# Four images of linear attention in one staggered stage, and the tally of clipped edges inside the fourth layer's stream

## The chip, the core and the metric

One core of a Trainium2 chip runs the whole program. The metric is the device time of one execution in microseconds. Engines are called TensorE (PE; its weight loads PEld), VectorE (DVE), ScalarE (ACT), GpSimd (POOL) and SyncE (SP, which only issues transfers here).

## The reference, cut to what matters

The input has 4 images of 128 channels by 32 x 32, which become 1024 tokens of 128 numbers each. Four layers follow one another; these lines of the reference carry the parts that the change touches:

```python
# third layer: linear attention, then a mixture
k = _inst_norm(k); v = _inst_norm(v)
dots = jnp.einsum('bhnd,bhne->bhde', k, v)
out = jnp.einsum('bhnd,bhde->bhne', q, dots) * (1.0 / n)
t = t + out_as_tokens @ w_out + b_out        # t: the tokens; q, k, v from _ln_t(t)
# fourth layer: attention over all tokens and in a window, then a graph attention
loops = jnp.arange(M, dtype=edge_index.dtype)
src = jnp.concatenate([edge_index[0], loops])
dst = jnp.concatenate([edge_index[1], loops])
e = jax.nn.leaky_relu(a_src[src] + a_dst[dst], negative_slope=0.2)
denom = jax.ops.segment_sum(ee, dst, num_segments=M)
agg = jax.ops.segment_sum(msg, dst, num_segments=M)
```

The graph attention has 524288 edges drawn over 32768 nodes, of which the kernel has M = 4096. A source beyond the last node is clipped to the last one, so the kernel doesn't handle such edges one by one: it counts, for each of its own nodes, how many clipped edges arrive there. That count is the tally. It depends on the edge list alone, not on any layer's values.

## The kernel before, in words

Each `stage` (L37) is a block of programs, one per engine, with semaphores of its own; all engines meet at its end. `loop` (L61) is a loop on the chip with barriers. Within a stage each engine runs its instructions strictly in the order written. `Beside` (L143) writes several programs into one engine's order by the turn numbers that they yield.

*Linear attention* (`linear_attention`, L1241, called in a loop over 4 images). Per image: `layer_norm` (L443: statistics, root, normalising on VectorE L464, transposes on TensorE), then keys and values of 8 token tiles (L1262, 128x512 each, a bank of PSUM for each of them), copied and squared on ScalarE (L1276, L1277), summed per head (L1285) and all 512 columns scaled (L1291) on VectorE, products of keys and values (L1268), then three `product_pass` stages: with the output weights (L1297), with the query weights (L1303), with the tokens (L1311) plus the bias as a product with a row of ones (L1312). VectorE adds the result to the tokens (L1315), and a second `layer_norm` follows. That is seven stages an image. After the loop come `mixture_weights` and `batch_normed_mixtures`.

*Fourth layer* (`fourth_layer`, L1552). A small stage first: POOL fills `f_v_ext` with ones (L1561) and reduces two counts over the partitions (L1562, L1565), VectorE fills a row of `f_stacks` and `f_pads` (L1570, L1571) and works out the number of laps, TensorE makes one column of bias (L1579). Then one long stage, `fourth_layer_stream` (L1589), for all images: 256 steps of two half steps. In a half step TensorE makes scores into a ring of two banks (L1825), VectorE takes their maximum (L2150), TensorE makes the transposed scores (L1849), ScalarE their exponential (L2033), and TensorE multiplies with the values (L1866). Beside them, at turn numbers (one turn is a half step, an image has 128), run `pre` of the next image (norm, queries, keys, values), `local` of this image (the windowed attention) and `tail` of the image before. `pre(0)` stands ahead of the stream: statistics on VectorE (L2053), root on POOL (L2188), normalising on ScalarE (L1901), products on TensorE (last L1710), roundings, and transfers to `f_stacks`. Then come the first 32 scores.

*Slots* (`take_in_slots`, L2945). POOL gathers 128 columns of rows by indirect transfers (L2816), in four groups of 32. ScalarE packs each group (L2826), and VectorE works through it as a band (`Taking.band`, L2834: from L2839 to L2878; 33 instructions). Between bands 1 and 2 come `Refill.place` (from L2934) and the start values (to L3053). The tally stands first in VectorE's and TensorE's order of this stage: the list of clipped edges, 1024 columns of two digits, is cut into 8 chunks of `TALLY` = 128; VectorE makes 64 one-hots a chunk (L3020, two chunks buffered), TensorE multiplies high by low digit, 128 products of 64x64 a chunk (L2985), and two copies, a product and a copy spread the counts (L3033, L2991, L3035). Then `Refill.draw` (L2921), the bands and the rest follow.

Of the kernel before, what the change touches and what calls it, by code (L numbers as in the profile page):

```python
# [1240 lines left out]
def linear_attention(nc, k, b):  # L1241

    with ExitStack() as c:
# [3 lines left out]
        G = 16  # L1247
        t_tm, xn, xc = k.t_tm[:, b], sb("l2_xn", [P, NT, P]), sb("l2_xc", [P, N])
        kv, sq = sb("l2_kv", [P, NT, 4 * P]), sb("l2_sq", [P, NT, 4 * P])
        st = sb("l2_st", [P, NT, G])  # L1250
        dots, mo, g = sb("l2_dots", [P, 2, P]), sb("l2_mo", [P, 2, P]), sb("l2_g", [P, P])
        ps = c.enter_context(psum(nc, "l2_ps", [P, 8, BANK], F32))
        layer_norm(nc, k, t_tm, xn[:], ps=ps, turned=xc)
        with stage(nc, "kv_ready", "copied", "squared", "chained", "rooted", "normed", "dots_ready", "masked") as (
                block, kv_ready, copied, squared, chained, rooted, normed, dots_ready, masked):
            def heads(x, t):
                return x[:, t].rearrange("p (g d) -> p g d", d=32)

            @block.tensor
            def _(pe):  # L1260
                for t in range(NT):
                    nc.tensor.matmul(ps[:, t], chunk(xc, t, P), k.w_kv[:], start=True, stop=True).then_inc(kv_ready, 1)  # L1262

                pe.wait_ge(squared, NT)
                for t in range(NT):
                    pe.wait_ge(normed, t + 1)
                    for i in range(2):
                        last = nc.tensor.matmul(ps[:, i, 0:P], kv[:, t, (2 + i) * P:(3 + i) * P],  # L1268
                                                kv[:, t, i * P:(i + 1) * P], start=(t == 0), stop=(t == NT - 1))
                last.then_inc(dots_ready, 1)  # L1270

            @block.scalar
            def _(act):
                for t in range(NT):
                    act.wait_ge(kv_ready, t + 1)
                    nc.scalar.copy(kv[:, t], ps[:, t]).then_inc(copied, 1)  # L1276
                    nc.scalar.activation(sq[:, t], ps[:, t], ACT.Square).then_inc(squared, 1)  # L1277
# [311 lines left out]
def fourth_layer_stream(nc, k, f, c):  # L1589
# [97 lines left out]
    def _(pe):  # L1687
# [154 lines left out]
        def scores_transposed(s, n):  # L1842
            h, m = steps[s]
            i = NC2 * s + n
            if m == 0 and n == 0:
                pe.wait_ge(rows_off, h + 1)
# [1429 lines left out]
```

## Time and profile before

| | us |
|---|---|
| three runs | 2886.87, 2897.33, 2886.83; median 2886.87 |
| the profiled execution | 2889.75, of which the span of the core 2888.0 |
| linear attention, four images | about 196 |
| small stage of the fourth layer | about 13 |
| opening, to the first score | about 52 |
| stream, image 0 from the first score | about 188 |
| slots | about 369 |

| engine | busy us | share of the span | instructions |
|---|---|---|---|
| PE | 1869.1 | 65% | 8280 |
| DVE | 1648.0 | 57% | 3684 |
| ACT | 966.2 | 33% | 1542 |
| POOL | 658.1 | 23% | 675 |

No engine is busy over the whole span; each stage has a limit of its own. Times in the profile are from the span's start. Matmuls are pipelined and their ends modelled, so TensorE's busy time is not time at its peak. Its clock has two levels, 1.2 and 2.4 GHz; "PEclk" is the granted share of the higher one.

### The profile page before, as it was taken

The numbers are of one execution on the slowest core, as the hardware profiler recorded it, in microseconds if no ns is written. First come the engines' busy times: TensorE is split into PE (matmuls) and PEld (weight loads), VectorE is DVE, ScalarE is ACT, GpSimd is POOL, SyncE is SP. The second block draws the span as 40 slices with busy tenths as digits, with TensorE's granted clock in tenths as the row PEclk, the third lists the DMA queues.
The fourth block names the chain that finished last, engine by engine and source line by source line (L and its number), as shares of the span: only waits on it lengthen the run. The fifth ranks groups of instructions, "written<-read, shape, count | busy, mean of one in ns | idle before, by whom it ended". The sixth has DMA issues, their size and how long they took to land. (4 is left out here: it accounts for less than half of the span.)

```text
span 2888.0 us, 25863 instructions
## 1 busy us (share of the span) xinstructions
PE 1869.1 (65%) x8280; PEld 825.4 (29%) x8280; DVE 1648.0 (57%) x3684; ACT 966.2 (33%) x1542; POOL 658.1 (23%) x675
## 2 busy tenths in 40 slices
PE   1564893785686666599658888787886410190089
PEld 1121321321221334456312223232222210090034
DVE  3485776767768654466545756656562121088823
ACT  1232141142132131255326675665664210000133
POOL 2200600420330300044312132332123157500000
PEclk7686896787888776699859999998897655555589
DMA  3301201201200000020021110110000021100030
GB/s 86 80 18 28 59 2 43 58 0 39 50 15 18 7 0 0 0 86 18 14 66 35 27 56 14 30 42 25 24 5 9 5 63 10 8 8 31 2 124 22
DMA packets 58242, 88.62 MB, mean 31 GB/s; under 512 B 17992, under 2 KB 29250, under 8 KB 57866
## 3 DMA queue, kind: packets, MB, share of 16 engines
q1 hardware_dynamic: 47604, 77.66, 9.0%
q10 hardware_dynamic: 6426, 7.99, 1.3%
q0 software_dynamic: 4096, 1.58, 0.8%
q8 instruction: 54, 0.88, 0.1%
q14 instruction: 62, 0.51, 0.1%
HBM read 58.59 MB, written 24.74 MB: 29 GB/s over the span
## 5 line engine op out<-in xcount | busy, mean ns | idle before, releaser
L2150 DVE TENSOR_REDUCE f_half_max<-f_ring 128x1 f32<-128x512 f32 x512 | 334.8, 684 | 306.3 <-PE f_ring L1825 304.1
L2033 ACT ACTIVATE f_probs<-f_ST 128x512 f32<-128x512 f32 x512 | 293.0, 597 | 212.4 <-PE f_ST L1849 208.2
L1825 PE MATMUL f_ring<-f_stacks 96*128 96x512 bf16 x512 | 212.7, 417 | 54.4 <-DVE f_half_max L2150 27.6
L772 DVE TENSOR_REDUCE att_half_max<-att_ring 128x1 f32<-128x512 f32 x256 | 161.1, 683 | 101.4 <-PE att_ring L659 92.7
L1849 PE MATMUL f_ST<-f_stacks 99*128 99x512 bf16 x512 | 203.8, 404 | 11.6 <-ACT f_probs L2033 11.6
L2985 PE MATMUL ts_ps<-ts_tally 128*64 128x64 bf16 x1024 | 97.5, 357 | 167.4 <-issue 145.3
L755 ACT ACTIVATE att_probs<-att_ST 128x1024 f32<-128x1024 f32 x128 | 129.4, 1024 | 155.8 <-PE att_ST L684 155.6
L3020 DVE TENSOR_SCALAR ts_tally<-ts_digits 128x256 bf16<-128x256 bf16 x512 | 77.4, 231 | 166.4 <-PE ts_ps L2985 112.8
L1459 POOL TENSOR_TENSOR bm_h<-bm_h,bm_mix 128x512 f32<-128x512 f32 x64 | 82.2, 1305 | 316.6 <-DMA bm_mix<-mix 229.5
L1866 PE MATMUL f_O<-f_probs,f_v_ext 128*32 128x512 f32 x1024 | 153.0, 673 | 0.0
L2985 PEld LDWEIGHTS ts_ps<-ts_tally 128*64 128x64 bf16 x1024 | 91.9, 263 | 172.9 <-issue 150.8
L684 PE MATMUL att_ST<-stacks 96*128 96x512 bf16 (+1 forms) x512 | 137.5, 397 | 0.0
L702 PE MATMUL att_O<-att_probs,v_ext 128*64 128x512 f32 x512 | 131.9, 641 | 6.6 <-DVE att_den L791 6.6
L659 PE MATMUL att_ring<-stacks 96*128 96x512 bf16 x256 | 104.3, 473 | 46.6 <-DMA stacks<-parts_dram 25.9
L2816 POOL DMA_INDIRECT ti_row<-features,slot_from x128 | 121.5, 949 | 56.6 <-issue 56.6
L1100 DVE TENSOR_TENSOR loc_weighed<-loc_wide,l_pad 128x512 f32<-128x512 f32 x200 | 124.4, 683 | 13.6 <-PE loc_wide L1054 8.6
L2359 PE MATMUL gm_ps<-xn_cm,x 128*128 128x512 f32 x128 | 62.5, 614 | 99.6 <-PEq L43 99.6
L1436 ACT ACTIVATE bm_h<-bm_ps,bn 128x512 f32<-128x512 f32 x128 | 99.6, 778 | 78.0 <-PE bm_ps L1403 72.7
L1825 PEld LDWEIGHTS f_ring<-f_stacks 96*128 96x128 bf16 x512 | 50.6, 99 | 259.6 <-DVE f_half_max L2150 163.6
L1082 POOL TENSOR_TENSOR loc_partial<-loc_partial,loc_weighed 128x512 f32<-128x512 f32 x88 | 110.1, 1272 | 9.9 <-DVE loc_weighed L1100 6.5
L1060 PE MATMUL loc_acc<-loc_weighed,turned 128*128 128x512 f32 x208 | 107.0, 598 | 0.4
L934 POOL MEMSET loc_padded<- 104x1296 f32 x4 | 4.7, 1178 | 446.7 <-POOLq L43 446.7
(546 smaller groups left out, 3419.6 us busy)
## 6 DMA issues: line engine op xcount, KB each, us to landing
f_stacks<-f_parts SPq DMA_DIRECT2D x192, 64.0 KB, 2.2
gates_wide<-gates SPq DMA_DIRECT2D x16, 512.0 KB, 12.3
parts_dram<-l_parts SPq DMA_DIRECT2D x8, 768.0 KB, 4.1
stacks<-parts_dram SPq DMA_DIRECT2D x24, 256.0 KB, 9.4
stacks<-parts_dram ACTq DMA_DIRECT2D x24, 256.0 KB, 10.6
f_parts<-f_parts SPq DMA_DIRECT2D x8, 768.0 KB, 3.5
es_raw<-L_ffn_edge_index SPq DMA_DIRECT2D x8, 512.0 KB, 4.7
bm_mix<-mix SPq DMA_DIRECT2D x8, 512.0 KB, 9.6
```

What stands on the lines that cost most here:

```text
L684: last = nc.tensor.matmul(ST[:, s % 2, n * BANK:(n + 1) * BANK], k.stacks[0:rows, 1, per * h + j, m * P:(m + 1) * P], k.stacks[0:rows, 0, ...
L702: last = nc.tensor.matmul(O[at:at + width, :], k.v_ext[:, m, h, :], probs[:, s % probs_ring, n * BANK:(n + 1) * BANK], start=(m == 0), sto ...
L755: nc.scalar.activation(probs[:, s % probs_ring, :], ST[:, s % 2, :], ACT.Exp).then_inc(probs_ready, 1)
L772: nc.vector.tensor_reduce(half_max[:, h % 2, t, n:n + 1], ring[:, i % RING], AX.X, ALU.max, negate=True).then_inc(reduced, 1)
L1100: nc.vector.tensor_tensor(o_, a, v, ALU.mult).then_inc(weighed_ready, 1)
L1825: nc.tensor.matmul(ring[:, i % RING], f.stacks[0:STACK, 0, at, t * P:(t + 1) * P], f.stacks[0:STACK, 1, at, n * BANK:(n + 1) * BANK], star ...
L1849: nc.tensor.matmul(ST[:, i % HALVES], f.stacks[0:STACK + 3, 1, h % HEADS, m * P:(m + 1) * P], f.stacks[0:STACK + 3, 0, h % HEADS, n * BANK ...
L1866: last = nc.tensor.matmul(O[at:at + 32, :], f.v_ext[:, h // HEADS % 2, m, h % HEADS, :], f.probs[:, s % PROBS, n * BANK:(n + 1) * BANK], s ...
L2033: nc.scalar.activation(f.probs[:, s % PROBS, n * BANK:(n + 1) * BANK], ST[:, i % HALVES], ACT.Exp).then_inc(probs_ready, 1)
L2150: nc.vector.tensor_reduce(f.half_max[:, h % 2, t, n:n + 1], ring[:, i % RING], AX.X, ALU.max, negate=True).then_inc(reduced, 1)
L2816: self.nc.gpsimd.indirect_dma_start(self.row[:, j, :], None, self.k.features, bass.IndirectOffsetOnAxis(ap=self.k.slot_from[:, j:j + 1], a ...
L2985: last = nc.tensor.matmul(ps[64 * a:64 * a + 64, 0, 0:64], low, high, start=(s == 0 and m == 0), stop=(s == chunks - 1 and m == TALLY // 2 ...
```

## The change

Linear attention of all images becomes one stage, `linear_attentions`, without the loop. Each image's program is written out for each engine with turn numbers from 0 to some 520, and the next image's begins 190 later; the engines' orders are merged by these numbers. Normalising is on ScalarE; keys and values use two banks of PSUM; key and value scales are multiplied, and only the key half is scaled; the bias is copied once to all partitions and added to the tokens by POOL.

The small stage of the fourth layer is dropped and its work put into the stream's stage: POOL fills `v_ext` first, then after `pre(0)` the row of `f_stacks`, the reductions, and, behind a wait for the first five chunks of the tally, `f_pads`.

The tally leaves the slots. Its first 640 columns are counted in five chunks of 128 in the opening: VectorE makes them behind its part of `pre(0)`, TensorE multiplies them in `first()`, behind `pre(0)` and ahead of the first score. The other 384 are counted in four chunks of 96 beside image 0, with one buffer. The core of the diff:

```diff
+class Linear:
+    STAGGER = 190
+    TURNED = (80, 500)
+    def start(self, program):
+        return Beside(*((b * self.STAGGER, program(b)) for b in range(B)))
...
+def linear_attentions(nc, k):
...
+                    if i >= 2:
+                        pe.wait_ge(kv_off, 2 * (i - 1))
+                    nc.tensor.matmul(kv_ps[:, i % 2], chunk(xc, t, P), k.w_kv[:], start=True, stop=True).then_inc(kv_ready, 1)
...
+                        last = nc.scalar.activation(f.xn[:, w, t, :], k.t_tm[:, b, t, :], ACT.Identity, bias=s[:, t, 2:3],
+                                                    scale=s[:, t, 1:2])
...
+                nc.gpsimd.tensor_tensor(x, x, f.bias[:].unsqueeze(1).broadcast_to([P, NT, P]), ALU.add).then_inc(biased.sem, 1)
...
+    EARLY, EARLY_TALLIES, LATE, LATE_TALLIES, LATE_TURNS = 128, 5, 96, 4, 28
...
+        def first():
+            for s in range(f.EARLY_TALLIES):
+                yield 22 + 2 * s
...
+                pe.wait_ge(hot_ready, 64 * (s + 1))
+                multiply(O, f.hot[:, s % 2], range(f.EARLY // 2), s == 0, s == f.EARLY_TALLIES - 1).then_inc(multiplied, 1)
+
+        def tally():
+            half, per = f.LATE // 2, 4
+            for s in range(f.LATE_TALLIES):
+                for g in range(half // per):
+                    yield f.LATE_TURNS * s + 15 + g
...
+        for s in range(f.EARLY_TALLIES):
+            if s >= 2:
+                dve.wait_ge(multiplied, s - 1)
+            one_hots(f.hot[:, s % 2], f.digits[:, :, s * f.EARLY:(s + 1) * f.EARLY], range(64))
...
+            per = 5
+            for s in range(f.LATE_TALLIES):
+                for g in range(0, 64, per):
+                    yield f.LATE_TURNS * s + 1 + g // per
...
+        split.wait(pool, 0)
+        nc.gpsimd.memset(f.stacks[STACK:STACK + 3, 1], 1.0).then_inc(made, 1)
...
+        pool.wait_ge(multiplied, f.EARLY_TALLIES)
+        nc.gpsimd.memset(f.pads[:], 0.0).then_inc(cleared, 1)
...
-            for s in range(chunks):
-                pe.wait_ge(hot_ready, 64 * (s + 1))
...
-                for v in range(64):
-                    nc.vector.tensor_scalar(hot[:, s % 2, :, :, v, :], here, float(v), None,
-                                            ALU.is_equal).then_inc(hot_ready, 1)
...
-            with loop(nc, 0, B) as b:
-                linear_attention(nc, k, b)
+            linear_attentions(nc, k)
```

## Rows read from the trace of the kernel before

**Rows 1.** Page, part 2: granted TensorE clock in 40 slices of 72.2 us.

```profile
PEclk7686896787888776699859999998897655555589
```

**Rows 2.** Busy by stage: PE, PEld, DVE, ACT, POOL us (instructions), clock, DMA share, GB/s.

```profile
1015.00:1211.00 196.00, 124.17 (x416) 81.17 (x416) 96.39 (x297) 48.54 (x96) 0.00 (x0) 0.67 0.00 0
...
1424.50:1477.00 52.50, 14.55 (x33) 7.01 (x34) 2.89 (x20) 12.25 (x20) 11.22 (x17) 0.50 0.15 47
1477.00:1665.00 188.00, 159.21 (x732) 41.51 (x732) 128.52 (x272) 105.82 (x191) 34.66 (x31) 0.88 0.13 36
...
2345.80:2714.90 369.10, 98.59 (x1028) 92.83 (x1028) 189.50 (x710) 13.18 (x13) 121.46 (x128) 0.50 0.11 21
```

**Rows 3.** Busy time by stretch: the first image of linear attention.

```profile
1015.00:1064.00 49.00, 30.78 (x104) 20.10 (x104) 24.37 (x75) 12.07 (x24) 0.00 (x0) 0.69 0.00 1
```

**Rows 4.** Groups of instructions, second image: busy us, mean ns, idle before them.

```profile
L1262 PE MATMUL l_ps<-w_kv,l_xc 128*128 128x512 f32 x16 | 8.5, 693 | 1.0 <-PEq L43 1.0
L1312 PE MATMUL l_ps<-rows,ones_row 1*128 1x128 f32 x16 | 6.0, 475 | 0.0
...
L1291 DVE TENSOR_TENSOR l_kv<-l_kv,l_st 128x512 f32<-128x512 f32 x8 | 4.9, 684 | 0.0
...
L464 DVE TENSOR_SCALAR l_xn<-t_tm,ln_s 128x128 f32 x16 | 4.3, 346 | 0.1
```

**Rows 5.** Timeline, fourth layer's opening: start, us, engine, line, operation [idle before].

```profile
1412.12 3.51 POOL L1561 MEMSET f_v_ext<- 128x4096 f32 x1 [3.29 <-ACTq L43]
...
1424.64 1.65 DVE L2053 BATCH_NORM_STATS2 f_moments_pre<-t_tm 128x6 f32<-128x128 f32 x8 [0.92 <-PEq L1582]
...
1432.06 0.20 POOL L2188 TENSOR_TENSOR f_norm_pre<-f_norm_pre 128x8 f32<-128x8 f32 x1 [10.01 <-issue]
...
1435.81 3.19 ACT L1901 ACTIVATE f_xn<-t_tm,f_norm_pre 128x128 f32<-128x128 f32 x8 [28.71 <-POOL f_norm_pre L2192]
...
1455.80 2.07 PE L1710 MATMUL f_side<-turned,xn_cm 128*128 128x128 f32 x8 [0.69 <-ACT f_v_ext L163]
...
1476.98 0.13 PEld L1825 LDWEIGHTS f_ring<-f_stacks 96*128 96x128 bf16 x2 [19.41 <-DMA f_stacks<-f_parts]
```

**Rows 6.** Busy time by stretch, in the slots.

```profile
2363.00:2426.00 63.00, 7.20 (x35) 4.94 (x33) 11.94 (x48) 2.10 (x1) 47.55 (x51) 0.50 0.15 10
2426.00:2526.00 100.00, 10.55 (x39) 7.39 (x40) 0.00 (x0) 0.00 (x0) 61.25 (x65) 0.50 0.12 8
2526.00:2603.00 77.00, 76.82 (x919) 76.61 (x918) 65.03 (x397) 0.00 (x0) 0.00 (x0) 0.50 0.05 19
```

**Rows 7.** Timeline of the slots.

```profile
2349.84 12.65 DVE L3020 TENSOR_SCALAR ts_tally<-ts_digits 128x256 bf16<-128x256 bf16 x80 [3.17 <-DMA ts_digits<-last_digits]
...
2389.03 2.10 ACT L2826 COPY ti_packed<-ti_row 128x768 f32<-128x768 f32 x1 [50.62 <-DMA ti_row<-features,slot_from]
...
2505.82 0.95 POOL L2816 DMA_INDIRECT ti_row<-features,slot_from  x1 [0.30 <-issue]
...
2539.02 8.81 DVE L3020 TENSOR_SCALAR ts_tally<-ts_digits 128x256 bf16<-128x256 bf16 x64 [1.95 <-PE ts_ps L2985]
...
2647.44 1.86 DVE L2934 TENSOR_REDUCE rf_fresh<-rf_drawn 128x32 f32<-128x1024 f32 x1
...
2668.00 0.42 DVE L2839 TENSOR_TENSOR ti_hot<-tiles,slot_tile 128x256 f32<-128x256 f32 x1
...
2714.37 0.23 DVE L2941 COPY slot_from<-rf_from 128x128 int32<-128x128 int32 x1
```

**Rows 8.** Busy time by stretch, in image 0 of the stream.

```profile
1517.00:1556.00 39.00, 32.62 (x162) 11.50 (x162) 18.58 (x36) 27.43 (x50) 6.38 (x3) 0.96 0.06 21
1556.00:1594.00 38.00, 34.16 (x182) 8.85 (x178) 22.43 (x43) 25.12 (x44) 13.10 (x6) 1.00 0.15 46
```

**Rows 9.** Busy time by stretch of L2033 alone, in image 0.

```profile
1556.00:1594.00 38.00, 18.25 (x32) 1.00 0.15 46
```

**Rows 10.** Groups of instructions, 1556 to 1665 us: one of POOL's.

```profile
L2213 POOL TENSOR_TENSOR f_prod<-f_lq,f_pads 128x1024 f32<-128x1024 f32 x5 | 11.0, 2210 | 9.1 <-PE f_side L1728 9.1
```

More of the change, by code:

```diff
@@ L1674, in fourth_layer_stream, with starts @@
     LAYER = [(0, 0), (1, 0), (0, 1), (1, 1)]
-    def starts(pre, local, tail):
-        programs = [(0, pre(0))]
+    def starts(pre, local, tail, first=None, tally=None, others=()):
+        programs = [(0, pre(0))] + ([] if first is None else [(0, first())])
+        head = len(programs)
+        if tally is not None:
+            programs.append((0, tally()))
+        programs.extend((0, other()) for other in others)
         for b in range(B):
@@ L1869, in mix @@
             last.then_inc(mixed_ready, 1)
-        before, beside = starts(pre, local, tail)
+        before, beside = starts(pre, local, tail, first, tally)
         before.finish()
@@ L1925, in pre @@
                 yield 20 + 2 * u
+                if b == 0 and u == 0:
+                    act.wait_ge(made, 1)
                 heads = f.v_ext[:, b % 2, 4 * u:4 * u + 4, :, 0:HD]
@@ new lines, in laps @@
+        def laps():
+            yield 10
+            dve.wait_ge(laps_reduced, 2)
+            count_laps(nc, k, linker(dve, laps_counted))
+        before, beside = starts(pre, local, tail, None, tally, (laps,))
+        before.finish()
+        for half in range(2):
+            r = slice(64 * half, 64 * half + 64)
+            nc.vector.tensor_copy(f.place[r, :], k.ident[r, r]).then_inc(tally_made, 1)
+        nc.vector.memset(f.total, 0.0).then_inc(tally_made, 1)
+        dve.wait_ge(digits_in, 32)
@@ L2169, in _ @@
+        dve.wait_ge(multiplied, f.EARLY_TALLIES)
+        for odd in range(2):
+            nc.vector.tensor_copy(f.total[:, odd, :, odd], O[:, 0:64]).then_inc(counted, 1)
         for s in range(len(steps)):
@@ L3030, in _ @@
             refill.place(dve, link, spread)
-            dve.wait_ge(multiplied, chunks)
-            for odd in range(2):
-                nc.vector.tensor_copy(total[:, odd, :, odd], ps[:, 0, 0:64]).then_inc(counted, 1)
-            dve.wait_ge(placed, 1)
-            link(nc.vector.tensor_copy(count[:], ps[:, 1, 0:MT]))
-            link(nc.vector.tensor_scalar(last[:, 0], count[:], 0.5, NEG, ALU.is_lt, ALU.mult))
+            link(nc.vector.tensor_scalar(last[:, 0], k.count[:], 0.5, NEG, ALU.is_lt, ALU.mult))
             for h in range(GH - 1, -1, -1):
```

420 lines of the change are left out of this document (289 added, 131 removed).

## The prediction, made before the changed kernel was run

> **What bounds the kernel now.** I read first where the granted clock is low (the page's slices), then the span by stage, then inside each stage the edit touches the timeline. The low-clock slices [rows 1] are the places where TensorE waits or does little: the linear attention, the opening of the fourth layer and the whole intake of slots. The stages give the sizes [rows 2]: linear attention 196 us, opening 52.5, first image 188, slots 369. No engine fills the first of these: an image takes 196/4 = 49.0 us, in which TensorE is busy 30.8, VectorE 24.4, ScalarE 12.1 [rows 3]; it is one chain, cut into seven small stages, in a loop. In the opening VectorE has 2.9 us of work in 52.5 [rows 2]. In the slots the tally is the plug: VectorE makes its one-hots ahead of everything else in its queue, and all four bands of slots come behind it. After 80 fast one-hots [rows 7] it gives out 48 in 63 us, and TensorE does 74 products and no more in 163 us [rows 6]; no wait on another engine is shown, and it ends some 20 us after the last gather is issued at 2505.82 [rows 7]. Then 919 products take 76.8 us [rows 6]. So the stage has three pieces in a row: tally beside the gather at a crawl, tally, bands.
>
> **Part 1, linear attention: -88 us.** Removed: the loop with its barriers, six stage boundaries an image, the bias products of each token tile (L1312, 6.0 us an image), half of the scaling (L1291, 4.9 us to about 2.8, since the two scales are multiplied) [rows 4]. Added: normalising goes from VectorE to ScalarE, twice 3.19 us [rows 5] against twice 2.15 [rows 4]; POOL adds the bias beside the keys and values, off the path (1024 columns took it 2.2 us elsewhere [rows 10]). The chain of one image: 49.0 - 6.0 - 2.1 + 2.1 - 5 for boundaries (the products of L1262 sat 1.0 us behind one of them [rows 4]; the rest is an estimate) + 2 for keys and values through two banks instead of eight, about 40 us. The next image starts 190 units of some 520 behind, which is 15 us of such a chain, so engines set the pace: ScalarE 12.1 + 6.4 = 18.5, VectorE 24.4 - 4.3 - 2.1 = 18, TensorE 30.8 - 6.0 = 24.8 at a clock of 0.67 to 0.69 and less when it is higher [rows 2 to 4]. I take 22. The stage: 40 + 3 x 22 + 2 to start = 108, against 196. Ends: 40 + 3 x 18.5 = 96 (-100); all at 1.2 GHz TensorE's 24.8 us become 24.8 x 0.67/0.50 = 33 an image, the chain about 46: 146 (-50).
>
> **Part 2, opening of the fourth layer: +19 us.** The small stage (13 us from the end of the mixtures at 1411.5 to 1424.6) goes. Its 3.5 us of filling v_ext [rows 5] stays on POOL ahead of the root, but the two all-reduces are moved behind; POOL's root began 7.4 us after VectorE's first statistics, with 10 us of idle before it that no wait explains [rows 5], and now can begin 4 us after. So TensorE's part of pre(0), which ended at 1457.9, ends at about 1412 + 33.3 - 3.5 = 1442. Now the tally: VectorE makes chunks 0 and 1 (64 x 0.138 = 8.8 us each [rows 7]) from 1416 to 1434, then waits for TensorE, which has first() behind all of pre(0) and ahead of the first score. A chunk of 128 products cost 76.8/919 x 128 = 10.7 us, and the clock stayed at 0.50 with TensorE busy without a gap [rows 6]; so five take 1442 + 53.5 = 1495.5, and the one-hots of the later chunks (8.8) fit beside. The first score comes at 1495.7 instead of 1476.98 [rows 5]: +19. If the clock were 1.0, VectorE would bind: 1442 + 5.3 + 3 x 8.8 + 5.3 = 1480, +3. High end +26: the root no earlier, and the stacks' row of ones (filled by VectorE before, now by POOL) in the way. SP issues two digit loads ahead of all its others; before, the one-hots began 4.0 us after their stage, so their load is short [rows 2, 7], and no stack load is due for 45 us. Queued behind POOL's new wait for the fifth chunk is the root of pre(1), not due before the stream has run six half steps: nothing.
>
> **Part 3, late tally beside image 0: +28 us.** 256 one-hots of 192 columns, between 0.103 and 0.138 us: 26 to 35 us of VectorE, and 384 products of 0.042 (half of the measured 0.084) to 0.084: 16 to 32 us of TensorE [rows 6, 7]. A half step, one exponential, takes 38/32 = 1.19 us [rows 9] with TensorE busy 34.2 of 38 and VectorE 22.4 [rows 8]. The one-hots come 5 to a half step in 13 of 28 half steps: 0.70 + 0.60 = 1.30 us, over 1.19, and the ring of two banks hands each delay to TensorE: 6 to 20 us over 52 half steps. The products, 8 to a half step over 48, find 10% slack, 6 us: 10 to 26. Together 16 to 46, I take 28; range 8 (busy figures overstate TensorE) to 60.
>
> **Part 4, slots: -180 us.** What is left for VectorE: the draw, two bands, the placing, the start, two bands. A band takes 46.4/2 = 23.2 us (2668.00 to 2714.37), placing and start 20.6 less 1.5 for the removed copies and product (2647.44 to 2668.00) [rows 7]. Band 0 can begin when ScalarE has packed it, 2389.0 + 2.1 = 2391 [rows 7]; bands 0 and 1 end at 2437, placing and start at 2457; band 2 waits for its gather, near 2469 + 2, and ends at 2494. Group 3 lands some 2.4 us after 2505.8 + 0.95 (group 0's last gather, 96 of 1.25 us earlier, ended at 2386.6, its pack began at 2389.0), is packed at 2511.3, and the last band's remaining 22.2 us end at 2534. The stage ended at 2714.6: -180. Late next is the gather itself. The stake is the crawl: VectorE then got one instruction in 63/48 = 1.3 us [rows 6]. It needs some 75 by the end of band 1 and had 80 ahead of the crawl; if all had to come at that rate, two bands of 33 take 66 x 1.3 = 86, placing and start 43 x 1.3 = 56, to 2533; two bands at speed follow: 2580, -134.
>
> By the Trainium skill ("Runtime: NRT & Kernel Launch", Instruction fetch mechanics) an engine holds 512 instructions, TensorE 2048, refilled in blocks, and a taken branch breaks the prefetch. No run here shows the buffer; the crawl after 80 instructions speaks for a fetch, and for rival C below.
>
> **Sum.** 2889.75 (the profiled execution, span 2888.0) - 88 + 19 + 28 - 180 = 2668.75; the median of the runs is 2.9 lower, so 2666.
>
> **The rivals.**
> A, as above: 2666. Chance 0.54.
> B, the tally holds TensorE at 1.2 GHz beside image 0. For it: 77 us without a gap left the clock at 0.50 [rows 6]. Against: the stream raised it to 0.96 by 1517 to 1556 [rows 8]. At half the clock 34.2 us of work in 32 half steps becomes 68: +0.97 us a half step, over the 48 with products +47: 2713. Chance 0.12.
> C, the crawl takes VectorE's bands: 2666 + 46 = 2712. Chance 0.13.
> D, POOL and VectorE block each other in image 0: POOL is busy 34.7 us there [rows 2], in ops of up to 2.2 us [rows 10]; if each that falls in the one-hots' 46% of half steps holds VectorE back, +16: 2682. Chance 0.08. The Trainium skill ("SBUF — State Buffer", Who interferes with whom) has tensor_scalar in its fast mode and POOL exclude each other for a whole instruction. Beside the gather 80 one-hots took 12.65 us, 0.158 each against 0.138 alone [rows 7]: a small cost, so the trace gives the rule little.
> E, the opening runs at full clock and the late tally hides: -16 - 20: 2630. Chance 0.07.
> F, the stagger doesn't overlap, because an in-order queue waits for the older image: 4 x 40 = 160 in part 1, +52: 2718. Chance 0.04. Against: the waits on older images are for buffers two images back or for banks long emptied.
> G, slower: the clock stays at 0.50 through the fourth layer's stream, since the tally both precedes and accompanies it. At 0.97 us a half step it eats the 221 us of gain after 228 half steps of 512, 1.8 images; for the whole stream +497: 3163. Against: the clock of [rows 8], and the tally ends within image 0. Chance 0.02.
>
> **How the numbers follow.** Range: A spreads by its own ends (about -35 and +45 combined), B, C, F lie inside 2740, E above 2625; so 2625 to 2740. 0.5% is 14 us, about what a measurement of this kernel can tell from no change; only G and rests of combined mishaps reach above 2872: faster 0.97, same 0.01, slower 0.02.
>
> **What would show it.** Part 1: from the first statistics of linear attention to the mixture weights near 108 us, one table load, ScalarE or TensorE busy over 80% in the middle. Part 2: five chunks 10.7 us apart at clock 0.50, first score 84 us after the end of the mixtures. Part 3: image 0 from 188 to some 216 us, and its clock (B). Part 4: first band right behind the first pack, last band ending 25 us after the last gather is issued; instructions spaced 1.4 us would be C. The forecast fails if the bands crawl and the clock drops together, or if the gather itself grows longer with bands beside it.

## The result and the profile after

The changed kernel takes 2757.34 us (median of 4 runs, 2752.18 to 2763.18) where the kernel before took 2886.85 (4 runs): ratio 0.9545, 95% interval 0.9526 to 0.9564. I had forecast 2666, with a range of 2625 to 2740. The direction was right; the gain was 130 us instead of 221, and the time lies outside the range. The profiled execution has a span of 2761.5 us against 2888.0. By stage, from the first statistics of linear attention to the choice of experts:

| stage | before | after | change | forecast |
|---|---|---|---|---|
| linear attention | 195.2 | 122.6 | -72.6 | -88 |
| mixtures | 200.4 | 201.1 | +0.7 | 0 |
| opening, to the first score | 65.5 | 86.7 | +21.2 | +19 |
| image 0, first score to its fourth group | 187.8 | 249.3 | +61.5 | +28 |
| images 1 to 3 | 561.9 | 567.7 | +5.8 | 0 |
| slots, last group to choice of experts | 491.2 | 349.4 | -141.8 | -180 |

This was not the whole result. On another chip the same two kernels gave 2726.75 us (10 runs) against 2734.46 (13 runs): ratio 0.9975, interval 0.9959 to 0.9991. Next to no gain is left there, and the experiments show why.

The page of the changed kernel, granted TensorE clock in 40 slices of 69 us, answers to [rows 1]; busy time by stretch, columns as in [rows 2], answers to [rows 2] and [rows 8]. In order: an image of linear attention, twice; the opening; its second half, with the tally alone; image 0 to its first group, and the rest of it.

```profile
PEclk7696787888689688799758989989989865555599
```

```profile
1040.00:1068.00 28.00, 17.18 (x85) 12.20 (x83) 17.86 (x57) 16.41 (x38) 3.01 (x2) 0.80 0.00 1
1068.00:1096.00 28.00, 17.18 (x82) 12.16 (x82) 17.80 (x57) 16.18 (x38) 2.34 (x1) 0.80 0.00 1
...
1338.00:1390.00 52.00, 35.84 (x286) 28.58 (x288) 32.59 (x198) 12.29 (x20) 23.79 (x20) 0.52 0.19 62
1390.00:1425.00 35.00, 32.91 (x393) 32.53 (x390) 20.18 (x149) 0.00 (x0) 11.75 (x2) 0.50 0.22 61
...
1425.00:1516.00 91.00, 75.79 (x340) 24.26 (x338) 65.04 (x208) 36.67 (x65) 11.18 (x17) 0.75 0.03 9
1516.00:1674.00 158.00, 138.06 (x784) 46.64 (x780) 105.89 (x326) 71.60 (x125) 26.01 (x15) 0.87 0.08 23
```

In the middle of linear attention no engine is busy for more than 18 of 28 us, so none of them sets the pace. VectorE's last copy of each of the four images (its timeline) shows how they follow one another:

```profile
1074.24 0.69 DVE L1470 COPY xn_cm<-l_turn 128x512 f32<-128x512 f32 x1 [0.22 <-PE l_turn L1301]
1102.75 0.69 DVE L1470 COPY xn_cm<-l_turn 128x512 f32<-128x512 f32 x1 [0.22 <-PE l_turn L1301]
1123.52 0.69 DVE L1470 COPY xn_cm<-l_turn 128x512 f32<-128x512 f32 x1
1136.09 0.69 DVE L1470 COPY xn_cm<-l_turn 128x512 f32<-128x512 f32 x1 [4.43 <-PE l_turn L1301]
```

The stage began at 1014.55, so the images end 60.4, 88.9, 109.7 and 122.2 us after its start. The opening's tally runs with a single gap, of 2.1 us, at clock 0.50, as [rows 6] had it. In image 0 TensorE has 213.9 us of work where it had 159.2 [rows 2], and its clock is low again for stretches.

The slots of the changed kernel, timeline of VectorE (start us, us, engine, line, operation, idle before and what ended it), answer to [rows 7]:

```profile
2408.29 1.23 DVE L3112 TENSOR_TENSOR ti_z<-ti_hot,ti_packed 128x1024 f32<-128x1024 f32 x1 [23.42 <-issue]
...
2449.07 1.23 DVE L3112 TENSOR_TENSOR ti_z<-ti_hot,ti_packed 128x1024 f32<-128x1024 f32 x1 [17.39 <-ACT ti_packed L3083]
...
2491.71 0.23 DVE L2993 TENSOR_SCALAR rf_from<-rf_whole 128x128 int32<-128x128 int32 x1 [1.16 <-DVE rf_whole L2992]
2493.12 0.26 DVE L2994 TENSOR_SCALAR rf_whole<-rf_whole 128x128 int32<-128x128 int32 x1 [1.18 <-DVE rf_from L2993]
2494.51 0.23 DVE L2995 CAST rf_f<-rf_whole 128x128 f32<-128x128 int32 x1 [1.13 <-DVE rf_whole L2994]
...
2541.69 0.43 DVE L3096 TENSOR_TENSOR ti_hot<-tiles,slot_tile 128x256 f32<-128x256 f32 x1
...
2588.09 0.23 DVE L3198 COPY slot_from<-rf_from 128x128 int32<-128x128 int32 x1
```

Band 0 and band 1 run at full speed as soon as they are packed; placing and start, between them and 2541.7, come for the most part one instruction in 1.40 us, although most of them take a quarter of a microsecond. I call that the crawl. The last gather is issued at 2525.6, the crawl ends some 13 us later, and bands 2 and 3 then stand behind it. That is rival C's cause in another place: C had bands 0 and 1 crawl too, and they didn't.

### The profile page after: what moved, and what is told of

It is laid out like the page before. It is cut to its first block and busy times, and to the rows that moved or that the text cites. A ratio compares the mean times of both kernels' runs of the same rounds, so it can differ in the third digit from the quotient of the medians.

```text
span 2761.5 us, 25395 instructions
## 1 busy us (share of the span) xinstructions
PE 1840.1 (67%) x8218; PEld 792.3 (29%) x8218; DVE 1628.0 (59%) x3680; ACT 990.0 (36%) x1604; POOL 693.1 (25%) x681
## 5 line engine op out<-in xcount | busy, mean ns | idle before, releaser
L2015 PE MATMUL f_ring<-f_stacks 96*128 96x512 bf16 x512 | 217.2, 425 | 44.8 <-DVE f_half_max L2351 38.7
L2061 PE MATMUL f_O<-f_probs,f_v_ext 128*32 128x512 f32 x1024 | 161.2, 706 | 0.1
L2015 PEld LDWEIGHTS f_ring<-f_stacks 96*128 96x128 bf16 x512 | 51.0, 100 | 250.1 <-DVE f_half_max L2351 167.2
L2617 PEld LDWEIGHTS gm_ps<-xn_cm,x 128*128 128x128 f32 x128 | 25.2, 198 | 306.7 <-issue 306.7
L2670 DVE TENSOR_TENSOR gm_h<-gm_h,gates_wide 128x1024 f32<-128x1024 f32 x32 | 39.2, 1226 | 98.3 <-ACT gm_h L2655 98.3
L912 PE MATMUL loc_ps<-loc_prod,place 128*32 128x512 f32 (+1 forms) x208 | 54.9, 688 | 32.8 <-DVE loc_prod L958 32.8
```

The lines of the kernel that those rows point to most:

```text
L2015: nc.tensor.matmul(ring[:, i % RING], f.stacks[0:STACK, 0, at, t * P:(t + 1) * P], f.stacks[0:STACK, 1, at, n * BANK:(n + 1) * BANK], star ...
L2061: last = nc.tensor.matmul(O[at:at + 32, :], f.v_ext[:, h // HEADS % 2, m, h % HEADS, :], f.probs[:, s % PROBS, n * BANK:(n + 1) * BANK], s ...
L2617: nc.tensor.matmul(ps[:, g % HIDDEN], k.x1[:, e, half * P:(half + 1) * P], chunk(k.xn_cm[:, b], n), start=True, stop=True).then_inc(hidden ...
```

## The experiments

The 18 runs below are in five groups, each on one chip with its own executions of the kernel before. A kernel without an interval was executed once. Times of stages are read from one profile each; a stage that an edit leaves alone came out within 1.5 us in nearly all of them (the opening at 86.4 to 86.8), but images 1 to 3 took 557 to 570 without a pattern. That kernel took 2730.89 in the first, 2734.46 in the second, and 2891.31, 2886.21 and 2890.86 us in the third to fifth. So there are chips where it takes some 2731 us and chips where it takes some 2888, and which it is matters more than the change. I call the second kind the chips with the crawl. No chip was used in two of the groups, so the chip and its state at that time can't be told apart.

### Group 1: image 0 taken apart (no crawl)

```diff
-                    last = multiply(x0.psum, f.hot_late, range(per * g, per * (g + 1)), s == 0 and g == 0,
-                                    s == f.LATE_TALLIES - 1 and g == half // per - 1)
+                    if g == 0:
+                        last = multiply(x0.psum, f.hot_late, range(per), s == 0, s == f.LATE_TALLIES - 1)
```

> Leaves out 88 of every 96 late products (352 of 384), so the edge counts are incomplete; all one-hots stay. Image 0 of the fourth layer (first score to the end of its fourth group) took 249.3 us in the changed kernel against 187.8 before, 61.5 more where I forecast 28. Theory: in the half steps with products TensorE is the bound, and eight products add their full 0.82 us (0.103 each, seen at full clock), so without them image 0 falls by some 36 us, to about 213. Rival one-hots: VectorE's bursts are the cost, and image 0 falls by under 10, to 240 or more. Rival clock: the low clock that lasted until the late tally's end comes from the products, and image 0 falls by over 45, to under 204.

```diff
-                    one_hots(f.hot_late, ..., range(g, min(g + per, 64)))
+                    if g == 0:
+                        nc.vector.tensor_scalar(f.hot_late[:, :, :, 0, :], here, 0.0, None, ALU.is_equal).then_inc(hot_ready, 64)
```

> Leaves out 63 of the 64 late one-hots of each chunk (the buffer is filled with zeros once by GpSimd), so the edge counts are incomplete; all 384 late products stay. Theory of TensorE's products: image 0 keeps most of its 61.5 us and falls by about 22 to 227. Rival one-hots: it falls by over 45, to 204 or less. If the one-hots hide wholly under TensorE it stays at 249.

> Leaves out both, 352 of 384 late products and 252 of 256 late one-hots. Both theories: image 0 comes back to the 187.8 us of before, give or take 4. If the two single runs gave falls that add up to this one's 61, they are independent costs; if they add to less, both must go for the time to come back. If it stays over 200, something else in the opening or the moved laps costs the rest.

Image 0 took 214.8 us without the products, 220.9 without the one-hots, 190.9 without both, against 249.3. The falls are 34.5, 28.4 and 58.4: nearly additive (62.9), so these are two costs of about the same size, and my 28 us held room for one. (Some 3 us stay: 190.9 is not 187.8.) Both "only products" and "only one-hots" are out. Busy time by stretch from the second group on, without the products, without the one-hots, without both (one row from each kernel):

```profile
1506.60:1636.60 130.00, 105.83 (x517) 26.76 (x516) 103.11 (x325) 70.19 (x126) 25.71 (x15) 0.89 0.10 28
```

```profile
1510.20:1643.60 133.40, 123.47 (x781) 45.03 (x780) 79.74 (x164) 71.13 (x126) 25.61 (x15) 0.99 0.10 28
```

```profile
1503.80:1615.00 111.20, 96.50 (x517) 25.92 (x516) 77.53 (x164) 69.74 (x126) 25.54 (x15) 0.98 0.12 33
```

With products and no one-hots the clock is 0.99; with one-hots and no products 0.89; with both 0.87. So the products don't hold the clock down, which refutes rival B as I had put it. The low stretches come with the one-hots, which make TensorE wait for its ring: in image 0 it sat idle for VectorE's maximum before its scores (L1825 before, L2015 after; idle times over 0.1 us summed) for 21.6 us with both and 24.4 without the products, and for 9.7 and 12.2 in the two kernels without the one-hots. Where the products lie, the timeline of TensorE in the changed kernel shows what they cost:

```profile
1535.71 0.89 PE L1919 MATMUL f_side<-f_hot_late 128*64 128x64 bf16 x8
1536.53 0.39 PE L2015 MATMUL f_ring<-f_stacks 96*128 96x512 bf16 x1
1536.76 0.38 PE L2042 MATMUL f_ST<-f_stacks 99*128 99x512 bf16 x1
1537.07 0.89 PE L1919 MATMUL f_side<-f_hot_late 128*64 128x64 bf16 x8
1537.89 0.39 PE L2015 MATMUL f_ring<-f_stacks 96*128 96x512 bf16 x1
```

Eight products take 1537.89 - 1537.07 = 0.82 us, 0.103 each at a clock of 1.00, more than the 0.084 that they took at 0.50 [rows 6], and a half step becomes 1.36 us. Part of that is the change from one kind of product to the other: the four pairs of the second row begin at 1537.07, 1537.28, 1537.44 and 1537.60, and the score 0.29 us after the last pair. Inside the row a pair takes 0.160 us, against 0.168 at half the clock. The 352 that were left out are 36 us, of which 34.5 reached the end: TensorE had next to no slack there.

```diff
-            for g in range(2):
-                t.band(dve, link, g, packed, shifted, exped, banded)
-            refill.place(dve, link, spread)
             (the start)
+            refill.place(dve, link, spread)
-            for g in range(2, BANDS):
+            for g in range(BANDS):
                 t.band(dve, link, g, packed, shifted, exped, banded)
```

> Slots: placing and start are moved ahead of band 0 on VectorE, into its 23.4 us of waiting for the first pack, with the start's exponential first on ScalarE; nothing is left out. Theory, crawl by count: VectorE gets about 80 instructions fast, whenever they come, and then one per 1.4 us until some 13 us after the last gather. Start, placing and band 0 (about 87 with the draw) are then fast, bands 1 and 2 crawl at 28 x 1.4 = 39 us each beside the gather and band 3 ends about 2530 + 30: the stage goes from 229 to about 200 us. Rival, crawl by place: it is the placing and start (many short instructions) that crawl wherever they stand; then they take 60 us from 2385, band 0 begins at 2445, and the stage takes 225 or more. Rival, crawl by time (it begins about 110 us into the gather whatever was issued): bands 0 and 1 are fast, band 2 crawls, stage about 195.

It took 2721.58 us, and from the first draw to the choice of experts 185.5. But the three kernels beside it that leave the slots alone took 186.0, 186.5 and 186.8 there, against 218.1 in the first profile of the changed kernel. No instruction had crawled in any of them, so this run said nothing on the order, and raised the question of the chip.

### Group 2: both kernels again (no crawl)

> The kernel before, unchanged, on a chip of its own choosing, for its profile. In the last experiments no instruction of VectorE crawled in the slots, and the kernel before took 2730.89 us there against 2886.85 in the first comparison. If the crawl belongs to the chip and not to the kernel: on a chip without it the one-hots of the tally run at 0.138 us each beside the gather, TensorE's products at 0.084, the stage of slots takes about 371 - 156 = 215 us, and all stages ahead of it are as before. If the 156 us lie elsewhere, a stage ahead of the slots is shorter.

> The changed kernel, unchanged, beside the kernel before on the same chip. If the crawl belongs to the chip: without it the slots take about 186 us (as in the three experiments that left that stage alone) and the whole some 2729, so against 2731 the change is worth nothing there, a ratio of 1.00; with it the ratio is 0.955 as in the first comparison. If it belongs to the kernels, the ratio is 0.955 on every chip.

The kernel before took 2723.23 us in its profiled execution. The stages up to the end of image 0 were as in the first profile (195.4, 200.1, 65.7, 187.6), and images 1 to 3 took 557.0 against 561.9; from the last group to the choice of experts it took 334.0 instead of 491.2. The changed kernel took 317.3 there. So where nothing crawls, moving the tally out of the slots saves 16.7 us, and it costs 21.0 in the opening and 62.8 in image 0. (By these two profiles alone the change loses 6 us, since images 1 to 3 differ by 13.1; the medians have it 7.7 ahead.) The slots of the kernel before, by stretch and in TensorE's timeline:

```profile
2363.00:2426.00 63.00, 63.00 (x761) 63.00 (x758) 58.95 (x383) 2.15 (x1) 51.42 (x39) 0.50 0.12 9
2426.00:2526.00 100.00, 12.33 (x140) 11.96 (x136) 89.37 (x162) 10.00 (x10) 72.91 (x71) 0.50 0.19 36
...
2351.62 85.64 PE L2985 MATMUL ts_ps<-ts_tally 128*64 128x64 bf16 x1024 [21.90 <-DVE ts_tally L3020]
```

All 1024 products run in one piece of 85.6 us beside the gather, where [rows 6] showed 74 in 163 us. There TensorE crawled too (its timeline, kernel before, first profile):

```profile
2385.39 0.27 PE L2985 MATMUL ts_ps<-ts_tally 128*64 128x64 bf16 x1 [2.53 <-issue]
2388.19 0.27 PE L2985 MATMUL ts_ps<-ts_tally 128*64 128x64 bf16 x1 [2.53 <-issue]
```

One product comes in 2.80 us. A product is two instructions, its weight load and itself, so that is 1.40 us an instruction again.

The tally lies beside the gather, but not for nothing. The gather took 181.9 us (2338.3 to 2520.2), against 160.2 in the crawl, and 166.7 in the changed kernel on this chip; 15.2 of the 16.7 us are this difference. Most of its calls still come 1.25 us apart, but two lasted as long as 64 one-hots. One of them, timelines of VectorE and GpSimd:

```profile
2394.61 8.81 DVE L3020 TENSOR_SCALAR ts_tally<-ts_digits 128x256 bf16<-128x256 bf16 x64 [0.63 <-PE ts_ps L2985]
...
2393.72 0.94 POOL L2816 DMA_INDIRECT ti_row<-features,slot_from  x1 [0.31 <-issue]
2394.97 8.58 POOL L2816 DMA_INDIRECT ti_row<-features,slot_from  x1 [0.30 <-issue]
2403.85 0.94 POOL L2816 DMA_INDIRECT ti_row<-features,slot_from  x1 [0.30 <-issue]
```

In these two chunks the one-hots ran at their full speed and a call waited them out (8.58 and 8.44 us instead of 0.95); in the others the calls kept their pace and 64 one-hots took 10.0 to 10.1 us. In the changed kernel the gather is the bound, and VectorE waits for the packs:

```profile
2363.00:2472.00 109.00, 0.00 (x0) 0.00 (x0) 53.06 (x74) 6.54 (x6) 83.39 (x85) 0.50 0.35 56
2472.00:2520.00 48.00, 0.00 (x0) 0.00 (x0) 37.63 (x88) 3.69 (x4) 36.99 (x37) 0.50 0.13 9
```

Up to 2472 this agrees with the first profile of the changed kernel (74 instructions against 72 in the same stretch); then 88 instructions come in 48 us where the other had 50 in 67.

```diff
-                for a in range(2):
-                    low, high = (hot[:, d, a, :, m] for d in range(2))
-                    last = nc.tensor.matmul(bank[64 * a:64 * a + 64, 0:64], low, high, ..., tile_position=(0, 64 * a))
+                low, high = (hot[:, d].rearrange("p a v m -> p (a v) m")[:, :, m] for d in range(2))
+                last = nc.tensor.matmul(bank[:, 0:P], low, high, ...)
```

> The tally's two products of 64x64 for a column (one for each half of the chunk, at two tile positions) become one of 128x128, whose two diagonal blocks are the same sums: 512 instead of 1024 products, one-hots unchanged, same result. Theory: a product costs its issue, 0.084 us in the opening and 0.103 beside the stream, with little for its columns; then image 0 falls by about half of 34.5, 17 us, and the opening's chunks cost 5.4 instead of 10.8 us of TensorE and are bound by VectorE's 8.8: about -8. Together 25 us less than the changed kernel. Rival: the cost is columns moved at 1.2 GHz (128 columns are 0.107 us), then the opening gains 0.168 - 0.107 = 0.06 a pair, hidden by VectorE, and image 0 gains as above if its clock is full. Rival no gain: weight load of 128 columns costs double, both stay.

2787.35 us, 2.1% more than the kernel before (ratio 1.0207, interval 1.0181 to 1.0233) and 60.6 us more than the changed kernel: +24.4 us in the opening and +37.2 in image 0. None of the three cases held. TensorE's timeline:

```profile
1366.19 80.78 PE L1918 MATMUL f_O<-f_hot 128*128 128x128 bf16 x320
```

One product of 128x128 takes 0.252 us at clock 0.50, two of 64x64 take 0.168. So halving the number of products is no way to make this tally cheaper: the price isn't the issue of an instruction. In the trace the two products of 64x64 of a pair, at their two tile positions, begin together, for the most part some 0.01 to 0.02 us apart. Whether the pair gains by that, or the 128x128 loses by its size or by the columns' stride in the one-hots, wasn't tried.

```diff
-                nc.gpsimd.tensor_tensor(x, x, f.bias[:].unsqueeze(1).broadcast_to([P, NT, P]), ALU.add)
+                nc.gpsimd.tensor_tensor(x[:, 0, 0:1], x[:, 0, 0:1], f.bias[:, 0:1], ALU.add)
```

> Linear attention: GpSimd's addition of the bias (1024 columns, 2.35 us an image) is cut to one column, so the output bias is missing from the tokens. In the changed kernel the 8-column scale on VectorE that falls beside it took 1.91 us where its twin took 0.17, and ScalarE's normalising waits 1.81 us for it, once an image. Theory of the shared port: the scale takes 0.2 us again, and the four images together end up to 4 x 1.8 = 7 us earlier (122.5 to about 116). Rival: the delay is off the path set by keys and values, and the stage stays within 1 us.

Linear attention took 119.1 us instead of 122.8, and all eight scales took 0.17. In the changed kernel, timelines of VectorE and of GpSimd:

```profile
1058.14 0.17 DVE L1426 SCALAR_TENSOR_TENSOR l_s<-l_s 128x8 f32<-128x8 f32 x1
...
1062.07 1.91 DVE L1426 SCALAR_TENSOR_TENSOR l_s<-l_s 128x8 f32<-128x8 f32 x1
...
1061.61 2.34 POOL L1480 TENSOR_TENSOR t_tm<-t_tm,l_bias 128x1024 f32<-128x1024 f32 x1 [20.94 <-ACT l_xn L1366]
```

The second scale ends at 1063.98, GpSimd's addition at 1063.95: it waited the addition out. That happened twice in the stage (1.91 and 1.90 us), not once an image as I had expected; two times 1.74 us are 3.5 of the 3.7 that the stage gained. At a stagger of 150 (below) none of the eight scales met an addition. The Trainium skill ("SBUF — State Buffer", Who interferes with whom) says that a VectorE instruction with two inputs in SBUF contends with a GpSimd instruction that reads SBUF; the trace agrees, 1.91 us against 0.17. I had looked for this contention in image 0 and not where the change puts a new GpSimd operation beside VectorE.

### Group 3: part 1 alone, and its stagger (crawl)

```diff
-            with loop(nc, 0, B) as b:
-                linear_attention(nc, k, b)
+            linear_attentions(nc, k)
```

> The kernel before with the staggered linear attention alone; tally, small stage and slots stay as they were. My forecast gave part 1 88 us; the profiles of the changed kernel show 72.6 fewer in that stage. Theory: the gain of that part reaches the end in full on any chip, 73 us less than the kernel before, since nothing downstream depends on it: about 2660 where the kernel before takes 2733 and no instruction crawls in the slots (ratio 0.973), about 2814 where it takes 2887. Rival: part of it is given back in the mixtures or the opening (another clock, another state of the queues), ratio over 0.98.

2817.13 us, ratio 0.9756 (0.9724 to 0.9788), 74.2 us less than the kernel before in the same group (2891.31), with the stage at 122.5. The first theory holds: part 1 reaches the end in full.

```diff
-    STAGGER = 190
+    STAGGER = 150
```

> Changed kernel with the images of linear attention 150 units apart instead of 190. If the order of the in-order queues sets the pace of 28.8 us an image (each engine is busy for only 16 to 23 of them), a closer stagger moves waits about and the stage changes by several us either way: up to 3 x 28.8 x (1 - 150/190) = 18 us shorter if the pace follows the stagger. If TensorE's work at its low clock sets the pace, it stays within 2 us of 122.7.

> The same with 240 units. If the pace follows the stagger, 3 x 28.8 x (240/190 - 1) = 23 us longer. If TensorE sets the pace, within 2 us of 122.7.

The stage took 107.5 us at 150 and 115.1 at 240, against 122.6 at 190. Both are shorter, so the pace neither follows the stagger nor is it TensorE's work: at 190 the images meet badly in the in-order queues (argued from these three times and the waits below; no run moved a single due time). At 150, by stretch:

```profile
1052.00:1075.00 23.00, 18.59 (x93) 12.88 (x92) 16.97 (x59) 16.56 (x41) 3.39 (x2) 0.93 0.00 1
```

ScalarE's first squares of the four images begin 15.2, 17.8 and 22.2 us apart, where the changed kernel has 19.0, 28.9 and 28.5. What the 190 units cost, TensorE's timeline of the changed kernel shows in one place:

```profile
1060.05 1.12 PE L1301 MATMUL l_turn<-ident,l_xn 128*128 128x128 f32 x4 [7.22 <-ACT l_xn L1366]
1064.63 2.08 PE L1323 MATMUL l_dots_ps<-l_kv 128*128 128x128 f32 x8 [3.47 <-DVE l_kv L1455]
```

TensorE waits 7.2 us for the normalising of one image and 3.5 for the scaling of another.

```diff
+            for _ in range(40):
+                link(nc.vector.memset(t.n[:, 0, 0, 0:1], 0.0))
             refill.draw(dve, link, pool_in, drawn)
```

> Changed kernel with 40 one-column fillings more on VectorE at the head of the slots, inside its wait for the pool of candidates. Where the kernel before takes 2887 (a place where instructions crawl): by the theory of a count of 80, band 0 would be the last fast one and bands 1, placing and start crawl, some 40 instructions at 1.4 us earlier; the slots grow by 15 to 40 us. Where the kernel before takes 2730 nothing crawls, and the stage stays at 186 us after the first wait, whatever the count.

The stage stayed at 218.2 us. The 40 fillings ran in 4.9 us while the gather was beginning (2350.5 to 2355.4), and the crawl began after some 105 instructions instead of some 75, ten instructions earlier in the program, at the end of band 1. So only a few of them counted; the test was badly placed and doesn't decide between count and time.

### Group 4: what the crawl hangs on (crawl)

```diff
-            for j in range(g * SLOTS, (g + 1) * SLOTS):
+            for j in range(g * SLOTS, g * SLOTS + 4):
                 self.nc.gpsimd.indirect_dma_start(...)
```

> Slots of the changed kernel with 4 of 32 gathers a band, the rest of the rows zeros, so most clipped edges are left out. Where the kernel before takes about 2890 (crawl): by the theory that the gather's own traffic slows the fetch of instructions, VectorE no longer crawls, and the stage is bound by VectorE's work, 10 for the draw + 4 x 23.2 + 20.6 = 124 us or, waiting for its inputs, up to 135. If instructions still come 1.4 us apart, the gather is not the cause. Where the kernel before takes 2730, nothing crawls and the stage is the same 124 to 135 against 197: then the gather is the bound of the stage in the changed kernel, by some 65 us.

125.9 us from draw to choice, on a chip where the kernel before took 2886: with 16 gathers instead of 128 nothing crawls. So the gather is needed for the crawl (one run). It isn't enough, since with all 128 calls the first two groups had no crawl.

> The kernel with start and placing ahead of band 0, again. Where the crawl occurs: crawl by a stock of some 80 instructions: start, placing and the first dozen of band 0 are fast, bands 0 to 2 take about 39 us each, and from the first draw to the choice of experts it takes 205 to 225 us against 218 of the changed kernel. Crawl by time (109 us after the gather's start): bands 0 and 1 fast, 190 to 200. Crawl of these instructions wherever they stand: over 225. Where nothing crawls: 185.5 as before.

2729.95 us in one run, with 194.8 from draw to choice against 218.1 (the first comparison) and 218.2 (the run with 40 fillings). VectorE's timeline:

```profile
2385.82 1.12 DVE L3260 SCALAR_TENSOR_TENSOR own_num<-ts_n,ts_last,own_num 128x32 f32<-128x32 f32 x4
...
2390.60 0.25 DVE L2982 SCALAR_TENSOR_TENSOR rf_code<-rf_fresh,band_low 128x32 f32<-128x32 f32 x1
2391.01 0.25 DVE L2983 SCALAR_TENSOR_TENSOR rf_code<-rf_code,band_low 128x32 f32<-128x32 f32 x1
2392.41 0.29 DVE L2989 TENSOR_SCALAR rf_f<-rf_code,bounds 128x128 f32<-128x128 f32 x1 [1.15 <-DVE rf_code L2983]
...
2395.90 0.23 DVE L2992 CAST rf_whole<-rf_f 128x128 int32<-128x128 f32 x1 [1.05 <-DVE rf_f L2991]
2397.30 0.23 DVE L2993 TENSOR_SCALAR rf_from<-rf_whole 128x128 int32<-128x128 int32 x1 [1.17 <-DVE rf_whole L2992]
```

The crawl now begins 38 us after the gather's start (2352.6) instead of 109, so it is no matter of time alone; the start ran fast, so it isn't these instructions. More instructions issued early bring it on early. But the stock is not a fixed 80: 83 instructions in the kernel before, some 75 with the old order, some 55 with the new one here and in one kernel below, some 30 in the other. Bands 0 to 2 beside the gather then took 44, 45 and 41 us (2402.2 to 2532.2; I had 39), and the last one ran fast. Without the crawl the same order took 185.5, so in this order the crawl costs 9 us and not 32: the packs come some 42 us apart in any case, and a crawling band takes little more.

Both combined kernels have the stagger of 150. In the one the tally is moved and start and placing come first, in the other the tally stays in the slots.

> The changed kernel with the stagger of 150 units and with start and placing ahead of band 0. Where nothing crawls: 2727 - 15 = 2712, ratio 0.992 to the kernel before, since the gather bounds the slots. Where it crawls: 2757 - 15 = 2742 and less what the new order gives in the run beside this one.

> The kernel before with the linear attention at a stagger of 150 units alone; tally, small stage and slots as they were. Where nothing crawls: 2734 - 73 - 15 = 2646, ratio 0.968, some 66 us under the moved tally, because there the tally lies beside the gather nearly for nothing. Where it crawls: 2817 - 15 = 2802, ratio 0.970, and slower than the moved tally.

2721.87 us (ratio 0.9419, 0.9378 to 0.946) and 2802.62 us (ratio 0.9714, 0.9691 to 0.9737). With the crawl the first beats both kernels of this study. The 81 us between the two are not the tally's alone, since the order differs too: the kernel with the tally moved, the stagger of 150 and the old order took 2744.36 (one run, in group 3), which leaves some 58 us for the tally and 22 for the order.

### Group 5: the same two (crawl)

> The kernel before with linear attention at a stagger of 150 alone, again. Where nothing crawls (kernel before at 2723 to 2739): 2734 - 90 = 2644, ratio 0.967. Where it crawls (kernel before at about 2886): 2802 as last time.

> The changed kernel with stagger 150 and start and placing ahead of the bands, again. Where nothing crawls: 2727 - 17 = 2710, ratio 0.991, some 66 us slower than the tally kept in the slots. Where it crawls: 2722 as last time, 80 faster than the tally kept.

The chip had the crawl again: 2801.81 (0.9706, 0.9679 to 0.9733) and 2722.87 (0.9436, 0.9408 to 0.9464), as in group 4. What the kernel with the tally kept takes without the crawl was not measured. An estimate from the stages above: 2734.46 - 72.6 - 15.1 = 2647 us, against 2712 for the moved one (2726.75 - 15.1).

## Why the prediction was wrong

- Part 1, -88, measured -72.6. That the gain reaches the end in full held, when the part ran alone. The sum behind it, a chain of 40 us and then 22 us an image, failed in both terms. The first image ended 60.4 us after the stage's start, since the others' instructions stand between its own, and the starts followed each other by 19.0, 28.9 and 28.5 us. I took the pace from the busiest engine and assumed that the written order would reach it. At 150 units the stage took 107.5, my 108, but that is luck: its first image took 60.1 too, and the others ended 22.9, 14.1 and 10.1 us apart. At the 190 of the change the order costs 15 us against that. [rows 3] and [rows 4] could not show this: the place to look was the due times in the new code, two images side by side.
- Part 2, +19, measured +21.2. Right, by its own steps: GpSimd's root began 4.3 us after the statistics, the tally ran at clock 0.50 and 0.084 us a product, and TensorE waited once, 2.1 us, for the one-hots of the third chunk. These took 12.72 us instead of 8.80: the first two, begun at 1379.9 and 1380.0, lasted 4.26 and 4.18 us, until GpSimd's fill of the stacks' row of ones (6.92 us) ended at 1384.03, and the rest ran at full speed. I had named that fill for the high end. The wait is read from the trace; no run left the fill out.
- Part 3, +28, measured +61.5, the second largest error. This step failed in both of its terms. I priced a product at 0.042 to 0.084 us, taking half of the measured 0.084 as the price at full clock. It was 0.103 at full clock (0.080 inside a row of eight), so the clock makes these products hardly cheaper, and [rows 6], all at 0.50, could not have told. And I subtracted 6 us of slack, where 34.5 of 36 us reached the end. The one-hots cost 28.4, above my 6 to 20, with the clock that they let fall. My upper end of 60 was just short. Rival D was not taken apart from the one-hots' 28.4. (Rivals B and G have 0.97 us a half step; by their own numbers, 68.4/32 - 1.19, it is 0.95, which changes neither.)
- Part 4, -180, measured -142.3 from the first gather to the choice of experts. The largest error, and the failed step is that placing and start take 20.6 us less 1.5: they took 69 us, from the end of band 1 to the start of band 2, instead of 19 where nothing crawls. I gave rival C 0.13. [rows 7] had the sign: after 80 fast instructions, all came at 1.3 us until the gather was over, and about 75 of the changed kernel's stood ahead of the placing. I read that as a stake narrowly won. But the placing and start come right behind these 75, and they are 53 instructions, not my 43. That C's -134 is near -142 is partly luck: it had bands 0 and 1 crawl, which ran fast, and band 1 begin without waiting for its pack, which it did for 17.4 us. On the chip without the crawl this part came nearly as forecast: 196.8 us from the first gather to the choice of experts, where 371.2 - 180 = 191.
- The sum. With the measured terms the forecast becomes 2668.75 + 15.4 + 2.2 + 33.5 + 37.7 + 6.5 (mixtures and later images) = 2764, which is the profiled execution's 2763.18. The 6.5 had no term of their own; they lie inside what images 1 to 3 vary by. Three terms were too good, and all three erred in the same direction. I combined the ends as if they were independent.
- The deeper error is one that the profile of one execution could not show. I took [rows 6] for what the kernel does. It is what the kernel does on some chips. On the others the tally was hidden under the gather for all but 17 us, which are mostly the calls that it holds up. Moving it is a loss of 84 - 17 = 67 us, which the 73 us of linear attention just make good: rival "the transfer hides it anyway", which I didn't write down, since 163 us of crawling stood before me.

## What to carry to other kernels

Work that lies beside a long transfer is priced by what the stage loses without it, not by its own time: the tally looked like the plug of the slots, and where VectorE is served normally it was worth 17 of its 86 us. Before half of a product's time is put down to the clock, find the same product at both clocks; these small ones were 5% cheaper at the higher one inside a row, and dearer with what stood around them. And when instructions come at a fixed spacing with no wait to explain it, run the kernel on more chips before moving work because of it. Where several programs are merged by due times, lay two of them side by side before the busiest engine is taken for the pace.

## What the runs showed of the hardware

- VectorE's instructions came one per 1.40 us (now and then 0.70 or 2.10) beside an indirect gather of 128 calls, in four of six groups of runs (each on one chip), after some 30 to 105 instructions since the gather began, until 8 to 20 us after its last call. TensorE was hit as well where it had work: in all four profiles that have both the crawl and the tally in the slots, 42 to 44 products with their weight loads came fast and then one in 2.80 us. In the two other groups there was none of it (2731 against 2888 us for the kernel before, 157 us). With 16 calls it was gone. The gather itself wasn't slowed: 1.25 us a call. The Trainium skill ("Runtime: NRT & Kernel Launch", Instruction fetch mechanics) tells of a buffer of instructions that is refilled; a stock that runs out fits with the onset, but no run shows the buffer, and the varying stock speaks against its being the whole story. What makes the chips differ stays open; no view of the profile that I read tells the two kinds apart ahead of the slots.
- A pair of products of 64x64 in bf16 at two tile positions took 0.168 us at clock 0.50 with nothing between, and 0.160 at 1.00 inside a row of four pairs; such a row between others took 0.82. One of 128x128 took 0.252 at 0.50.
- VectorE and GpSimd waited each other out for whole operations. Beside an addition of 2.34 us on GpSimd an 8-column operation of VectorE took 1.91 us instead of 0.17; beside a fill of 6.92 us on GpSimd the first of 64 one-hots took 4.26 us and ended with it; and twice a call of the gather took 8.4 to 8.6 us instead of 0.95 beside 64 one-hots at full speed. Beside calls that kept their pace 64 one-hots took 10.0 to 10.1 us instead of 8.8.
